# The queries' stack transfers are issued by ACT's queue instead of SP's, in a decoder layer on one core

## What is computed

```python
x = _layernorm(x + _L0_attn_ref(x, A, B, W, b))          # a linear recurrence over the tokens
x = _layernorm(x + _L0_xattn_ref(x, ctx, ctx, Wq, ...))  # attention, 16 heads of 16, band of +-50 tokens, RoPE
x = _layernorm(x + _L0_ffn_ref(x, router_w1, ...))       # 16 experts, each takes its best 64 tokens of a batch
...
q = q * cos + _rotate_half(q) * sin
k = k * cos + _rotate_half(k) * sin
scores = jnp.einsum("bhqd,bhkd->bhqk", q, k) / np.sqrt(D_K)
scores = jnp.where(dist <= WINDOW, scores, -1e9)
p = jax.nn.softmax(scores, axis=-1)
out = jnp.einsum("bhqk,bhkd->bhqd", p, v)
```

## Time and profile before

| | |
|---|---|
| Median of three runs | 1283.4 us (1279.87 to 1285.6) |
| The profiled execution, its own time | 1285.46 us |
| Its span, first to last instruction | 1283.7 us |
| Mean granted clock of PE | 0.929 of full speed |
| PE busy over the span | 1076.8 us (84%) |
| DVE, ACT, POOL busy | 672.2 (52%), 531.7 (41%), 667.9 (52%) |
| Packets of SP's queue (q1) | 62322, 81.96 MB |
| Packets of ACT's queue (q10) | 1136, 0.51 MB |

### The profile page before, as it was taken

One profiled execution on the slowest core, in us unless ns is written; L12 is line 12 of the kernel. 1 busy time (PEld: TensorE's weight loads), 2 busy tenths in 40 slices (PEclk: granted clock), 3 DMA queues, 4 the chain that ended last, 5 costly groups with the idle time before them and its releaser, 6 DMA issues. The chain is left out here.

```text
span 1283.7 us, 22405 instructions
## 1 busy us (share of the span) xinstructions
PE 1076.8 (84%) x6564; PEld 900.9 (70%) x6564; DVE 672.2 (52%) x2184; ACT 531.7 (41%) x1179; POOL 667.9 (52%) x808
## 2 busy tenths in 40 slices
PE   5688888788888888886319999999999999999990
PEld 3566667566667676664217888888888888888880
DVE  4466666566666666553355444354445444444437
ACT  1143444344444444433214445444555444444431
POOL 5345555455554555533032665556565665556544
PEclk9889999899999999978659999999999999999995
DMA  5644445445553444330433544455544544445338
GB/s 139 96 67 67 75 75 84 66 79 83 84 85 65 75 76 76 48 54 18 140 113 101 108 75 95 107 110 110 102 107 106 114 85 76 108 107 115 50 55 257
DMA packets 88128, 117.16 MB, mean 91 GB/s; under 512 B 10977, under 2 KB 63330, under 8 KB 87906
## 3 DMA queue, kind: packets, MB, share of 16 engines
q1 hardware_dynamic: 62322, 81.96, 29.1%
q0 software_dynamic: 24576, 33.57, 15.9%
q10 hardware_dynamic: 1136, 0.51, 0.2%
HBM read 65.41 MB, written 29.36 MB: 74 GB/s over the span
## 5 line engine op out<-in xcount | busy, mean ns | idle before, releaser
L1075 POOL DMA_INDIRECT acc_rows<-y,slots_now x128 | 209.4, 1636 | 186.6 <-ACT y L1205 164.7
L602 ACT ACTIVATE probsT<-scoreT 128x356 f32<-128x356 f32 x256 | 118.4, 463 | 287.5 <-PE scoreT L468 287.3
L719 DVE CUSTOM_DVE_ANT_0 scored<-score,band 128x178 f32<-128x178 f32 x512 | 153.1, 339 | 140.5 <-PE score L440 134.8
L1267 DVE TENSOR_TENSOR hidden<-gate,value_bank 128x512 f32<-128x512 f32 x128 | 87.9, 687 | 253.3 <-ACT gate L1214 242.8
L1056 POOL DMA_INDIRECT rows<-x_rows,rows_now x128 | 137.9, 1077 | 59.6 <-issue 46.1
L1214 ACT ACTIVATE gate<-gate_bank 128x512 f32<-128x512 f32 x128 | 76.5, 598 | 221.6 <-PE value_bank L1112 221.6
L440 PE MATMUL score<-k_stack,q_stack 96*128 96x178 f32 x512 | 125.0, 328 | 49.0 <-DMA q_stack<-low_q 32.9
L1112 PE MATMUL y_bank<-w_hi,h_hi 128*128 128x256 f32 x512 | 146.6, 286 | 0.0
L440 PEld LDWEIGHTS score<-k_stack,q_stack 96*128 96x128 f32 x512 | 94.0, 203 | 73.2 <-issue 56.3
L1112 PE MATMUL y_bank<-w_hi,h_lo 128*128 128x256 f32 x512 | 144.4, 282 | 0.0
L1112 PE MATMUL y_bank<-w_lo,h_hi 128*128 128x256 f32 x512 | 144.1, 281 | 0.0
(11 more groups left out here) (149 smaller groups left out, 2328.0 us busy)
## 6 DMA issues: line engine op xcount, KB each, us to landing
raw<-in_w SPq DMA_DIRECT2D x48, 512.0 KB
k_stack<-high_k SPq DMA_DIRECT2D x64, 128.0 KB, 4.1
q_stack<-high_q SPq DMA_DIRECT2D x64, 128.0 KB, 5.3
xT<-in_xT SPq DMA_DIRECT2D x16, 256.0 KB, 2.8
xin<-in_x SPq DMA_DIRECT2D x16, 256.0 KB, 3.1
cT<-in_cT SPq DMA_DIRECT2D x16, 256.0 KB, 3.7
k_stack<-low_k SPq DMA_DIRECT2D x32, 128.0 KB, 5.5
q_stack<-low_q SPq DMA_DIRECT2D x32, 128.0 KB, 6.0
```

What stands on the lines that cost most here:

```text
L602: nc.scalar.activation(probsT[g % 2][:, u % HG, :, :].rearrange("p a s -> p (a s)"), scoreT[u % 2][:, 0:2 * SPAN], ACT.Exp, scale=1.0 / DH ...
L719: op = nc.vector.tensor_tensor_reduce(scored[t % 2][:, q, :], score[t % 2][:, q * SPAN:(q + 1) * SPAN], band[:, q, :], -1.0, BIG, ALU.add, ...
L1075: nc.gpsimd.indirect_dma_start(dram["acc"][c], bass.IndirectOffsetOnAxis(ap=slots_now[it.r % 2][:, c:c + 1], axis=0), y[m][:], None, compu ...
L1267: nc.vector.tensor_tensor(hidden[f % 2][:], gate[f % 2][:], value_bank[f % 2][:], ALU.mult).then_inc(hidden_ready, 1)
```

## The change

The queries' six stack transfers leave SP's program and enter ACT's. SP's function now does only the keys. ACT issues the four of `high_q` directly behind `heighten(it, 1)` at t = 10, after it waits for its own copy to be complete, and the two of `low_q` at t = 12, behind the exponentials of that position, after a wait for POOL's low_q. The same semaphore counts them (`stacked[1]`), and the waits on PE are as before. The first use also waits for the cleared buffers (`fixed_set`), as SP did once at its start.

```diff
-            def stack(it, which):
+            def stack_keys(it):
...
                 maxima(it, 0)
                 if there(it, "K"):
-                    stack(it, 0)
+                    stack_keys(it)
                 maxima(it, 1)
-                if there(it, "Q"):
-                    stack(it, 1)
                 if there(it, "O"):
...
+            def stack_queries(it, kind):
+
+                par = (it.r + 1) % 2
+                part, landed = (high, high_ready) if kind == "high" else (low, low_ready)
+                if kind == "high":
+                    if it.at_least(1):
+                        act.wait_ge(scoreT_ready, it.lin(NH, 0))
+                    if not it.at_least(0):
+                        act.wait_ge(fixed_set, FIXED)
+                act.wait_ge(landed[1], it.lin(1, 2))
+                for c in range(3):
+                    if PARTS[1][c] == kind:
+                        for a in range(2):
+                            rows = slice(STACK * a + DH * c, STACK * a + DH * c + DH)
+                            src = part[1][64 * a:64 * a + 64].rearrange("p f s -> p (f s)")
+                            act.dma_start(q_stack[par][rows, a].rearrange("d (k f) s -> d k (f s)", f=KT).bitcast(F32),
+                                          src.bitcast(F32)).then_inc(stacked[1], 16)
...
                     if t == 10 and there(it, "Q"):
                         heighten(it, 1)
+                        stack_queries(it, "high")
+                    if t == 12 and there(it, "Q"):
+                        stack_queries(it, "low")
```

More of the change, by code:

```diff
@@ L287, in stack @@
                 for kind, part, landed in (("high", high, high_ready), ("low", low, low_ready)):
-                    sp.wait_ge(landed[which], it.lin(1, 2))
+                    sp.wait_ge(landed[0], it.lin(1, 2))
                     met()
                     for c in range(3):
-                        if PARTS[which][c] == kind:
+                        if PARTS[0][c] == kind:
                             for a in range(2):
                                 rows = slice(STACK * a + DH * c, STACK * a + DH * c + DH)
[L294 to L297, removed]
+                                src = part[0][64 * a:64 * a + 64].rearrange("p f s -> p (f s)")
+                                sp.dma_start(k_stack[par][rows].rearrange("d (k f) s -> d k (f s)", f=KT).bitcast(F32),
+                                             src.bitcast(F32)).then_inc(stacked[0], 16)
             def step(it):
```

## The result

| | before | after |
|---|---|---|
| Median of the runs | 1283.2 us (1279.9 to 1285.6, 4 runs) | 1319.1 us (1315.3 to 1322.3, 4 runs) |
| Ratio | | 1.028, 95% interval 1.024 to 1.032 |
| Profiled execution, span | 1285.5, 1283.7 | 1315.3, 1313.5 |
| First logits of the router (end of `mixing`) | at 619.77 | at 649.58 |
| From there to the end of the span | 663.9 | 663.9 |

The changed kernel is slower by 35.9 us in the medians. In the two profiled executions the difference of the spans is 29.8 us, and all of it lies in `mixing`.

The account below looks back on a forecast made before the run. The prediction took the maxima of group 1, landing through full transfer engines, to start the chain setting each batch. Delay 2.0 less slack 0.2 gave 1.8 us, times 14 +25 us on 1283.4: 1308 us, range 1280 to 1330.

Parts of the forecast that it names:

- main case: First stage: late maxima of group 1 cost 1.8 us a batch, +25 us, 1308 us; chance 0.66 together with rival C.
- The maxima of group 1 are what starts a batch's chain, and the queries' wait is beside it: Batch boundary: the maxima start L466 at t = 14, then 6.30 us to x1's transposes; the queries' wait, 2.29 us, lies beside.
- The transfer engines are full, so earlier issues do not shorten the line: Stack loads: engines move 123 GB/s, 1.07 us per 128 KB transfer, so earlier query issues do not shorten the line.
- Rival A: Stack loads: the two queues overlap by ports or the delay stays within slack; 1280 to 1288 us, centre 1283; chance 0.18.
- The delay of the maxima: 2.0 us: Key loads: 1.9 query transfers of 1.07 us run before the last key, delaying the maxima 2.0 us, less 0.2 slack.
- rival C: Key loads: equal sharing of queues delays the maxima 3.4 us, 3.2 a batch, up to 1330 us; chance 0.66 with main case.
- The delay passes whole to the next batch: From t = 14 on: 1.8 us a batch passes whole through the 6.30 us chain to x1's transposes and everything behind.
- Rival B: PE behind the boundary: clock may stay at 2.4 GHz, worth 1.6 us a batch, -21 us, 1262 us; chance 0.10.
- At the loop's jump the delay comes on top: Where PE is held about 6 us at the loop's jump, the delay adds to it, because PE's own last matmuls move.
- ACT pays nothing: ACT's six added issues: cost on the path 0, bounded above by 0.8 us a batch.
- rival D: ACT: costly issues or late low_q make exponentials hold PE, up to 0.8 us a batch, +11, 1294 us; chance alone 0.06.
- The fill: Before the first batch, no maxima in line: first stacks may end sooner, by at most 3.6 us, as rival A allowed.

Follow-up runs that it names:

- e3: Kernel before, with SP issuing the six query transfers ahead of the maxima of group 1 and ACT issuing nothing; 1348.1 us, ratio 1.053.
- e5: Changed kernel, with ACT issuing high_q one position later, at t = 11, and low_q still at t = 12; 1294.6 us, ratio 1.011.
- e2: Changed kernel, with ACT issuing high_q at t = 12 instead of t = 10 and low_q at t = 13 instead of t = 12; 1282.6 us, ratio 1.003.
- e7: Kernel before, with PE's projection of the keys' input put ahead of a batch's first score instead of behind the transposes of x1; 1247.5 us, ratio 0.973.
- e1: Changed kernel, with SP issuing the maxima of group 1 behind the first two key transfers instead of all six; 1298.2 us, ratio 1.014.
- e9: e7 with ACT's log_Y and guess_Y ahead of the exponentials of t = 14 instead of behind them; 1246.3 us, ratio 0.971.

## Why the prediction was right, and where its steps were off

The forecast was 1308 us, slower, with a range to 1330; measured were 1319.1. The direction, the place and the mechanism are those of its main case. Of its steps:

- **The maxima of group 1 are what starts a batch's chain, and the queries' wait is beside it.** Right. e3 lengthens the time by 5.3% with 78.8 us of that wait, and removing 27.9 us of the queries' wait gained nothing. One premise held only in part: in two steps of the kernel before, from 300.03 and from 440.83 us, the last key lands 10.0 us behind the first key issue and L466 starts at 9.5, so the maxima can land ahead of the last key.
- **The transfer engines are full, so earlier issues do not shorten the line.** Right: 117 GB/s with two queues, and the last query lands 15.77 us behind the first key issue in the step shown, 15.02 before. Rival A, overlap by ports, fell: the key and query transfers write different partitions, and the rate did not rise. It would have given about 1283. "SBUF — State Buffer", section "Can I just issue two DMAs to hit both halves?", in the Trainium skill says that two concurrent transfers gained only 6% over one; the trace agrees and shows no gain at all.
- **The delay of the maxima: 2.0 us. This term failed.** Between the first key issue and L466 of t = 14 there were 309.57 - 300.03 = 9.54 us before and 327.16 - 313.53 = 13.63 after, so t = 14 starts 4.1 later. The prediction took the delay of the last key for the delay of the maxima. The delay of the last key it had nearly right, 2.4 us for 2.0 in the step shown above, though by two errors that cancel: it let 3.2 key transfers share with the queries at 0.6 to 1, and in that step two of them share at one to one, so that 2 query transfers land before the last key where it had 1.9. (In four of the thirteen steps the last key is 3.3 to 3.5 us late.) What it put at nothing is the longer time from the last key to the maxima:

| step | last key lands | t = 14 starts | between |
|---|---|---|---|
| before, from 368.50 (waits 0.28) | 9.1 | 9.98 | 0.9 |
| e5, from 337.40 (waits 1.62) | 9.1 | 11.34 | 2.2 |
| after, from 350.44 (waits 3.95) | 11.4 | 13.66 | 2.3 |

In the twelve other steps of the changed kernel from 85.13 to 537.98 the time between is 1.6 to 2.8, before 0.6 to 1.1 where PE waits. In e3, where the maxima stand behind six queries on one queue, it is 0.1 to 0.6 from the last query. So a second full queue holds the small transfers back beyond what it does to the large ones ahead of them. Why is not settled. The 3.4 that rival C has for equal sharing is nearer to 4.1, but it places the whole delay on the keys, and in nine of thirteen steps the keys show 2.2 to 2.4.

- **The delay passes whole to the next batch. Half right.** The rows for one step of each kernel, first of before, then of after:

```profile
309.57 0.33 PE L466 MATMUL scoreT<-band_bf,ident_bf 128*128 128x356 bf16 x1
...
315.78 0.66 PE L506 MATMUL work<-ident,x 128*128 128x128 f32 x4
```

```profile
327.16 0.48 PE L463 MATMUL scoreT<-band_bf,ident_bf 128*128 128x356 bf16 x1 [3.90 <-DMA q_stack<-nmaxT]
...
333.66 0.55 PE L503 MATMUL work<-ident,x 128*128 128x128 f32 x3 [0.45 <-DVE x L761]
```

| stretch of the step | before | after | difference |
|---|---|---|---|
| first key issue to L466 of t = 14 | 9.54 | 13.63 | +4.09 |
| L466 to the transposes of x1 | 6.21 | 6.50 | +0.29 |
| transposes to the next first key issue | 18.43 | 16.78 | -1.65 |
| key issue to key issue | 34.18 | 36.91 | +2.73 |

(Key issues at 300.03 and 334.21 before, 313.53 and 350.44 after.) The first difference passes through the chain of x1, as forecast. The last row but one was not forecast: 1.65 us come back. The granted clock of the rows fits it. Windows behind and around the boundary, first before, then after:

```profile
315.80:319.80 4.00, 4.00 (x16) 3.49 (x16) 1.48 (x10) 2.14 (x5) 0.42 (x1) 0.57 0.01 2
319.80:334.20 14.40, 14.07 (x105) 11.89 (x104) 10.49 (x48) 6.35 (x19) 9.21 (x11) 1.00 0.20 57
```

```profile
326.30:333.00 6.70, 5.84 (x30) 4.08 (x30) 1.08 (x6) 1.75 (x6) 2.76 (x8) 0.50 0.22 57
333.00:350.40 17.40, 16.62 (x119) 14.09 (x119) 12.34 (x60) 8.47 (x24) 9.58 (x11) 1.00 0.15 46
```

Before, PE ran mostly at the 1.2 GHz level (0.57) right behind its wait for the queries, with 4 us of its own work to do. After, the low level comes behind the new wait, 6.7 us of it, in a stretch where x1's chain on POOL and DVE sets the pace; behind the transposes the clock is 1.00. Rival B's price, 1.6 us a batch, was paid out after all in such a step, inside the slow case. It is not paid in every one. In the steps from 85.13, 124.97 and 350.44 the low stretch lasts 10 to 14 us and reaches beyond the transposes, and the next key issue follows them by 18.3 to 19.6 us, as late as before or later. A line of the step from 350.44:

```profile
373.00:374.00 1.00, 1.00 (x4) 0.71 (x4) 0.00 (x0) 1.00 (x3) 0.00 (x0) 0.51 0.00 0
```

So this pair of steps is one of the shortest. Over thirteen steps the mean from key issue to key issue is 37.67 us after (85.13 to 574.90) and 34.91 before (88.90 to 542.71), 34.18 without the two steps that hold a stall. 1.8 us a batch was forecast; 2.8 came in the profiled executions, 3.5 beside the steps without a stall. That the forecast of 1308 came as near to 1319.1 as it did is in part luck: t = 14 is late by 4.1 instead of 2.0, and the clock, put at 0, gave back up to 1.65.
- **At the loop's jump the delay comes on top.** Wrong for these two profiles. Before, PE stands 6 us there in two places (the earlier trace rows leave them out), one of them here, and in the changed kernel nowhere:

```profile
387.35 0.70 PE L440 MATMUL score<-k_stack,q_stack 96*128 96x178 f32 x2 [5.82 <-issue]
```

```profile
407.77 0.72 PE L437 MATMUL score<-k_stack,q_stack 96*128 96x178 f32 x2
```

The last section looks at what goes with it. The two steps before take 39.73 and 38.14 us instead of 34.2, so the stalls hide some 9 us of the loss in the profiles. That fits a difference of 29.8 there beside 35.9 in the medians, but the other executions have no profile, and it is not shown.
- **ACT pays nothing.** Right where the change puts the issues: four cost 2.75 us (2.56 on SP), and PE reaches the wait for the maxima as early as before (9.16 and 9.15, see e3). e2 shows 12.6 us more of PE's waits for ACT with the issues two positions later, so rival D is a matter of the position.
- **The fill.** The first score of batch 0 starts 3 us earlier (40.68 against 43.74), but this is not the gain that rival A named. SP's first key issue is already 3.05 us earlier (25.12 against 28.17), before any query is issued, and the last query lands 15.4 us behind it in both kernels. In the eleven profiles this first issue lies between 25.1 and 30.0 us; why it moves no run here shows. So of the 29.8 us another 3 of loss are hidden.

## What to carry to other kernels

Before a transfer is moved to another queue, look whether the transfer engines are full at that time; if they are, a second queue does not make the whole land earlier, it only changes who stands in front of whom, and a 2 KB transfer at the end of the other queue may wait for half a megabyte (four query transfers of 128 KB here). The largest wait in the list is a wrong target when another chain ends within a tenth of a microsecond of it: follow the chain that the next instruction waits for as well. Where two such chains tie, give the waiting engine independent work (e7, -35 us, part of it perhaps the clock that no longer falls) before shortening either.

## What the runs showed of the hardware

- **Two full queues share the transfer engines one packet to one** (207 to 218), and together reach 117 GB/s for transfers onto 16 partitions, no more than one queue alone (123). In the step shown whole transfers of the two queues land in turns. "DMA: Bandwidth & Descriptors", section "Queues, rings and completion order", in the Trainium skill says that an engine takes turns between the queues it has work for; the trace agrees.
- **Small transfers at the end of a queue can wait longer than the large ones ahead of them when a second queue is full.** PE's start at t = 14 follows the landing of the last key by 2.3 us in the changed kernel and by 2.2 in e5, where the keys are not late at all, against 0.9 on one queue.
- **A wait can move the clock's low stretch to where it costs less.** The low level lasted longer in the changed kernel (6.8 us in ten of thirteen steps, 10 to 14 in the other three; 3.4 before, where no stall stands), yet in the ten the stretch behind the transposes became 1.2 to 2.1 us shorter than the 18.3 of before.
- **Work in place of a wait can keep the clock up.** In e7 the stretch at the 1.2 GHz level is gone in 11 of 14 steps.
- **The stall of 6 us at the loop's jump goes with instruction packets in the loop.** Of eleven profiles three have it (before, e1, e9), and just these three have 42 packets of queue q8, all others 24. Lines of the page, before and after:

```profile
q8 instruction: 42, 0.69, 0.3%
```

```profile
q8 instruction: 24, 0.39, 0.1%
```

The packets more lie in the second and third pass of the loop. From 231 to 510 us the kernel before has

```profile
q8 instruction: 18, 0.29, 0.6%
```

and the changed kernel none there, up to 550 us. Two of the 18 start at 240.7 and one at 245.5, around the first stall (239.0 to 245.2). In the window from 245 to 460 the three profiles have 13 to 15 packets and the eight others none. What decides whether they are there is open. e9's profiled execution, with two stalls of together 11.8 us, took 1255.5, the highest of its four runs (1242.3 to 1255.5), which would fit a stall that comes and goes within one kernel. e1's, with 13.9 us of stalls, lies in the middle of its four (1297.3 to 1300.6), and there is one profile of each kernel, so it is not shown. It limits what a single profile can say here to some 9 us, the estimate above from the two long steps.
